# Experts on rows sorted by expert, between the two halves of the shared units

## The reference

```python
g = x @ sw1.T                                   # shared: 1024 hidden
u = x @ sw2.T
shared_out = jax.nn.silu(g) * u @ sw3.T
scores = jax.nn.sigmoid(x @ router_w.T)         # 8 experts
_, top_idx = jax.lax.top_k(scores + expert_bias, 2)
top_scores = jnp.take_along_axis(scores, top_idx, axis=-1)
top_scores = top_scores / (top_scores.sum(-1, keepdims=True) + 1e-09)
combine = jnp.zeros((T, E), x.dtype).at[jnp.arange(T)[:, None], flat_idx].add(flat_sc)
h12 = jnp.einsum('td,ehd->teh', flat_x, w12)    # 8 experts, 128 hidden each
h1, h2 = jnp.split(h12, 2, axis=-1)
out_e = jnp.einsum('teh,edh->ted', jax.nn.silu(h1) * h2, w3)
return shared_out + jnp.einsum('ted,te->td', out_e, combine).reshape(b, s, d)
```

## Time and profile before

| | |
|---|---|
| median of 3 runs | 1283.42 us (1282.84 to 1287.9) |
| profiled execution | 1282.67 us |
| its span, first to last instruction | 1280.9 us |
| TensorE (PE) busy | 1195.8 us, 93% |
| VectorE (DVE) busy | 958.9 us, 75% |
| ScalarE (ACT) busy | 577.9 us, 45% |
| GpSimd (POOL) busy | 198.2 us, 15% |
| mean granted TensorE clock | 0.962 of 2.4 GHz |

### The profile page before, as it was taken

The page is one execution under the profiler, slowest core; times in us unless marked ns, Lnnn a source line. Parts: engine busy times, 40 slices in busy tenths (PEclk is TensorE's granted clock), DMA queues, the critical chain, the costliest instruction groups (busy, mean ns, idle before and its releaser), DMA issues.

```text
span 1280.9 us, 22138 instructions
## 1 busy us (share of the span) xinstructions
PE 1195.8 (93%) x7800; PEld 798.3 (62%) x7800; DVE 958.9 (75%) x1964; ACT 577.9 (45%) x1194; POOL 198.2 (15%) x154
## 2 busy tenths in 40 slices
PE   5789999999889999999897799999999799999998
PEld 4334444444578888888783344444435688888887
DVE  7898888883558777777886688888845687777776
ACT  6236666666432232222262266676674222322322
POOL 4440000000301222222152000000003022222220
PEclk9769999999989999999987699999999899999999
DMA  3621111100100000000049423233101000000001
GB/s 127 150 41 36 36 36 36 36 12 11 61 7 26 25 25 25 25 25 0 6 119 177 58 43 65 62 66 63 23 11 59 1 26 25 25 25 25 24 0 65
DMA packets 34893, 54.59 MB, mean 43 GB/s; under 512 B 11231, under 2 KB 25503, under 8 KB 32465
## 3 DMA queue, kind: packets, MB, share of 16 engines
q1 hardware_dynamic: 31877, 41.57, 13.3%
q10 hardware_dynamic: 2940, 12.05, 4.0%
HBM read 40.94 MB, written 11.99 MB: 41 GB/s over the span
## 4 chain that ended last, share of the span: by engine, by line
PE 77%; DVE 12%; DMA 3%; ACT 2%; issue 2%; POOL 2%; SPq 1%; ACTq 0%; DVEq 0%
PE o_ps L627 11%; PE st_ps L611 10%; PE st_ps L157 8%; PE st_ps L158 8%; PE st_ps L159 8%; PE su_ps L587 6%; DVE mab L969 4%; PE st_ps L587 3%; PE o_ps L157 3%; PE su_ps L157 3%; PE o_ps L159 3%; PE su_ps L159 3%; PE o_ps L158 3%; PE su_ps L158 3%; PE st_ps L614 2%
## 5 line engine op out<-in xcount | busy, mean ns | idle before, releaser
L834 ACT ACTIVATE pt<-st_ps 128x512 f32<-128x512 f32 (+3 forms) x768 | 333.3, 494 | 225.9 <-PE st_ps L614 112.9
L611 PE MATMUL st_ps<-qs,ks 99*128 99x512 bf16 (+7 forms) x768 | 246.4, 332 | 12.2 <-DMA qs<-nmx 6.9
L157 PE MATMUL st_ps<-xt_h,wu_h 128*128 128x512 f32 x512 | 201.9, 394 | 0.0
L158 PE MATMUL st_ps<-xt_h,wu_l 128*128 128x512 f32 x512 | 201.1, 393 | 0.0
L159 PE MATMUL st_ps<-xt_l,wu_h 128*128 128x512 f32 x512 | 199.5, 390 | 0.0
L969 DVE TENSOR_REDUCE mab<-su_ps 128x1 f32<-128x512 f32 (+2 forms) x288 | 182.3, 659 | 21.0 <-PE su_ps L591 14.7
L856 ACT CAST hh<-hf 128x512 fp32r<-128x512 f32 x128 | 79.3, 620 | 227.3 <-DVE hf L1114 227.3
L1116 DVE TENSOR_TENSOR hl<-hf,hh 128x512 fp32r<-128x512 f32 x128 | 103.7, 810 | 87.8 <-ACT hh L856 87.8
L587 PE MATMUL su_ps<-ks,qs 96*128 96x512 bf16 (+5 forms) x448 | 162.5, 376 | 1.7 <-DVE mc L969 0.6
L627 PE MATMUL o_ps<-pt,vp 128*32 128x512 f32 (+3 forms) x1536 | 163.2, 498 | 0.0
L853 ACT ACTIVATE sg<-st_ps 128x512 f32<-128x512 f32 x128 | 76.5, 598 | 154.2 <-PE st_ps L159 154.2
(11 more groups left out here) (146 smaller groups left out, 1968.0 us busy)
## 6 DMA issues: line engine op xcount, KB each, us to landing
wr<-w_units_dram SPq DMA_DIRECT2D x32, 384.0 KB, 3.1
qs<-q_parts ACTq DMA_DIRECT2D x60, 128.0 KB
q_parts<-hml SPq DMA_DIRECT2D x16, 384.0 KB, 3.6
qs<-q_parts SPq DMA_DIRECT2D x36, 128.0 KB
inv<-inverses SPq DMA_DIRECT2D x128, 32.0 KB, 1.9
ks<-k_parts ACTq DMA_DIRECT2D x30, 128.0 KB
k_parts<-hml SPq DMA_DIRECT2D x8, 384.0 KB, 2.5
ks<-k_parts SPq DMA_DIRECT2D x18, 128.0 KB
```

The source lines that it names most:

```text
L157: pe.matmul(out, lh, rh, start=n == 0, stop=False)
L158: pe.matmul(out, ll, rh, start=False, stop=False)
L611: last = pe.matmul(bank[KM_BANKS[n % len(KM_BANKS)]][:, lo - CH * part:hi - CH * part], key_stack(l, s)(j)[0:rows, P * kt:P * kt + P], qs[ ...
L834: act.activation(pt[:, kt % 2, j, lo:hi], bank[KM_BANKS[i % len(KM_BANKS)]][:, lo - CH * part:hi - CH * part], ACT.Exp, scale=1 / np.sqrt( ...
```

## The change

Experts are no longer computed on all tokens. In each feed-forward:
- The steps go over chunks 0 and 1 for all 8 shared units (16 steps), then the routed part, then chunks 2 and 3 for the 8 shared units (16 steps). `down` accumulates over the 8 units in PSUM; `add_shared` adds the sum to `xs` once.
- `route` also ranks every (token, expert) pair: a count by matmul (`count_ranks`), running sums on VectorE, and so `pos`, the slot of each pair in a list in which every expert begins on a tile of 128. 4096 pairs and 8 partly filled tiles fit into 40 tiles, taken as 20 pairs of tiles (`SPAIRS`). `offset` gives the column of each tile's expert in the weights.
- POOL scatters the normalised rows into `slots` in DRAM with 32 indirect DMAs (16 tiles of tokens, 2 experts), and after the routed part gathers the rows of `outs` with 32 more; VectorE's `combine` adds each times its `share`.
- The routed part loads a pair of tiles (256 KB), transposes it, splits it, multiplies it with the weights of the experts that a register points to, applies silu and product, transposes the hidden part, splits it, multiplies again and stores the result (256 KB).
- The weights are split once, by POOL in the first attention (`keep_units`), and kept in DRAM as two parts; SyncE loads a shared unit (768 KB, ring of three) for each two steps, and both parts of all experts (6.3 MB) in each feed-forward.
- `vp` shares its place with the experts' weights, and is set to ones again by POOL after the first routed part.

The diff, cut to what the prediction speaks of:

```diff
@@ SyncE
+            def load_slots(f, i):
+                n = SPAIRS * f + i
+                if i >= 3:
+                    sp.wait_ge(rtr_done, n - 2)
+                sp.dma_start(rows_in[:, n % 3, :, :], slots_v[i]).then_inc(slots_in[n % 3], 16)
+
+            def send_outs(f, i):
+                n = SPAIRS * f + i
+                sp.wait_ge(ry_done, n + 1)
+                sp.dma_start(outs_v[i], rows_out[:, n % 3, :, :]).then_inc(outs_out[n % 3], 16)
...
+                sp.wait_ge(slots_out, 16 * 2 * TT * (f + 1))
+                for i in range(3):
+                    load_slots(f, i)
+                load_unit(f, SHARED + 2)
+                for i in range(SPAIRS):
+                    if i + 3 < SPAIRS:
+                        load_slots(f, i + 3)
+                    send_outs(f, i)
@@ POOL
+                for n in range(UNITS):
+                    pool.wait_ge(raw_in[n % 2], 16 * (n // 2 + 1))
+                    wait(pool, unit_kept, 16 * n)
+                    pool.tensor_tensor(stage[:, 0, :], wraw[:, n % 2, :], zero[:, :].to_broadcast([P, WIDTH]), ALU.subtract).then_inc(stage_step, 1)
+                    pool.wait_ge(stage_step, 2 * n + 1)
+                    pool.tensor_tensor(stage[:, 1, :], wraw[:, n % 2, :], stage[:, 0, :].bitcast(F32), ALU.subtract).then_inc(stage_step, 1)
+                    pool.wait_ge(stage_step, 2 * n + 2)
+                    pool.dma_start(unit_parts[n], stage[:, :, :].bitcast(F32)).then_inc(unit_kept, 16)
...
+            def scatter(f):
+                pool.wait_ge(pos_done, f + 1)
+                for t in range(TT):
+                    c, r = divmod(t, TC)
+                    for j in range(2):
+                        pool.indirect_dma_start(slots, bass.IndirectOffsetOnAxis(ap=pos[:, j, t:t + 1], axis=0),
+                                                normal_rows(1, c)[:, r, :], None).then_inc(slots_out, 16)
@@ TensorE
+                def turn_rows(i):
+                    n = SPAIRS * f + i
+                    pe.wait_ge(slots_in[n % 3], 16 * (n // 3 + 1))
...
+                    for a in range(2):
+                        for k in range(KE):
+                            last = pe.transpose(bank[n % 2][:, 2 * P * k + P * a:2 * P * k + P * a + P],
+                                                rows_in[:, n % 3, a, P * k:P * k + P], ident)
+                    last.then_inc(rtr_done, 1)
+
+                def up_rows(i):
...
+                    for a in range(2):
+                        at[2 * i + a] = pe.value_load(offset[0:1, 2 * i + a:2 * i + a + 1], min_val=0, max_val=WIDTH * (NEXP - 1))
+                    pe.wait_ge(rxl_done, n + 1)
+                    wait(pe, rh_done, n - 1)
+                    for a in range(2):
+                        ts = slice(P * a, P * a + P)
+                        w = at[2 * i + a]
+                        last = split_product(pe, bank[2 + n % 2][:, E * a:E * a + E], [
+                            (rx_h[:, n % 2, k, ts], rx_l[:, n % 2, k, ts], wexp_h[:, bass.ds(w + E * k, E)], wexp_l[:, bass.ds(w + E * k, E)])
+                            for k in range(KE)])
+                    last.then_inc(rup_done, 1)
...
+                for k in range(SPAIRS + 3):
+                    if k < SPAIRS:
+                        turn_rows(k)
+                    if 0 <= k - 1 < SPAIRS:
+                        up_rows(k - 1)
+                    if 0 <= k - 2 < SPAIRS:
+                        turn_hidden(k - 2)
+                    if k >= 3:
+                        down_rows(k - 3)
@@ ScalarE
+                def take_rows(i):
+                    n = SPAIRS * f + i
+                    act.wait_ge(rdown_done, n + 1)
+                    wait(act, outs_out[n % 3], 16 * (n // 3))
+                    act.copy(rows_out[:, n % 3, :, :].rearrange("p a e -> p (a e)"), bank[6 + n % 2]).then_inc(ry_done, 1)
@@ VectorE, end of a feed-forward
+                while taken < 2 * TT:
+                    combine(f, taken)
+                    taken += 1
                 if f == 0:
+                    stats(2, 0)
+                    stats(2, 1)
                     normalise(2, 0)
-                add(f, UNITS // 2 - 1, 7)
+                add_shared(f, 2)
+                add_shared(f, 3)
+                if f == 0:
+                    stats(2, 2)
+                    normalise(2, 1)
+                    stats(2, 3)
```

More of the change, by code:

```diff
@@ L48 @@
 NEXP = 8
-UNITS = 16
-FS = UNITS * NCH
+SHARED = 8
+UNITS = SHARED + NEXP
+FS = SHARED * NCH
+RING = 3
+SPAIRS = (2 * T // P + NEXP) // 2
+SLOTS = 2 * SPAIRS * P
+GBUFS = 8
+COMBINE_BEHIND = {e: 2 for e in range(19, 32)}
+WIDTH = 3 * E
+ROUTE = 2 * TT + 32
 EPS = 1e-5
@@ L297, in tr_bank, with normal_rows, unit_turn, place @@
             return bank[4 - banks + i % banks], i - banks if i >= banks else None
+        def normal_rows(p, c):
+            return xn2[:, c - 2, :, :] if p % 2 and c >= 2 else xn[:, c % 2, :, :]
+        def unit_turn(f, n):
+            return divmod(2 * SHARED * f + n, RING)
+        def place(e):
+            pair, r = divmod(e, 2 * SHARED)
+            return r // 2, 2 * pair + r % 2
+        def outs_count(n):
+            return [16 * len(range(b, n, 3)) for b in range(3)]
         def batch_parts_out(l, b, n):
@@ L421, in attention, with load_unit @@
                     sp.dma_start(wfc[:, :, :], fc_b).then_inc(wfc_in, 16)
[L423 to L427, removed]
+            def load_unit(f, n):
+                turn, r = unit_turn(f, n)
+                if n >= RING:
+                    sp.wait_ge(down_done, FS * f + 2 * (n - RING + 1))
+                sp.dma_start(wu[:, r, :, :].bitcast(F32), unit_parts[n % SHARED]).then_inc(unit_in[r], 16)
@@ L495, in _, with feed_forward @@
+            def feed_forward(f):
+                rstds(2 * f + 1)
+                scatter(f)
+                gather(f)
+            pool.wait_ge(ones_set, 2)
             rstds(0, 0, 1)
@@ new lines, in feed_forward @@
+            def feed_forward(f):
+                for e in range(2, 2 * SHARED):
+                    if e == 5:
+                        count_ranks(f)
+                    up(f, e)
+                    if e == 2:
+                        down(f, 0)
+                    down(f, e - 1)
+                down(f, 2 * SHARED - 1)
+                routed(f)
+                for e in range(2 * SHARED, FS):
+                    up(f, e)
+                    if e > 2 * SHARED:
+                        down(f, e - 1)
+                down(f, FS - 1)
@@ L1110, in hidden @@
+            def hidden(f, e):
+                s = FS * f + e
                 a = e % 2
@@ L1130, in experts, with add_shared @@
-            def experts(f):
-                for e in range(8):
-                    hidden(f, 0, e)
-                    if e:
-                        add(f, 0, e - 1)
-                    route(f, e)
-                last = UNITS // 2 - 1
-                with dve.Fori(1, last) as i:
-                    for e in range(8):
-                        hidden(f, i, e)
-                        if e:
-                            add(f, i, e - 1)
-                        else:
-                            add(f, i - 1, 7)
-                for e in range(8):
-                    hidden(f, last, e)
-                    add(f, last if e else last - 1, (e - 1) % 8)
-                    if f == 0 and e in STATS_AT:
-                        stats(2, STATS_AT.index(e))
+            def add_shared(f, c):
+                pair, r = divmod(c, 2)
+                dve.wait_ge(down_done, FS * f + 2 * SHARED * (pair + 1) - 1 + r)
+                if pair:
+                    dve.wait_ge(combined, 2 * TT * f + 2 * TC * (c + 1))
+                for half in range(2):
+                    t = TC * c + 2 * half
+                    rows = xs[:, t:t + 2, :].rearrange("p t e -> p (t e)")
+                    dve.tensor_tensor(rows, bank[4 + 2 * r + half], rows, ALU.add).then_inc(shared_added, 1)
```

501 lines of the change are left out of this document (361 added, 140 removed).

## The result

The changed kernel takes 1445.58 us (median of four runs, 1444.97 to 1449.12) where the kernel before takes 1283.13 in the same place: ratio 1.127, 95% interval [1.125, 1.129]. Its profiled execution took 1446.15 us, span 1444.2. The forecast was 1388, its 8-in-10 range 1300 to 1450.

The account below looks back on a forecast made before the run. TensorE, 93% busy, bounds the kernel before; SyncE's load-behind-send order would pace routed turns. Feed-forwards +92, tails +11.5 and splitting +2 give +105.5 us, 1388 us; forecast alone 1350 to 1430, 8 in 10 1300 to 1450.

Parts of the forecast that it names:

- The order on SyncE paces each turn: Routed part: row loads queue behind sends of results four pairs back, so sixteen turns per feed-forward pay a full round trip.
- L: Routed turn's round trip: copy with hand-overs 0.7 us, store issue 0.35, row load 3.0; sum 4.05 us, ends 3.2 and 5.2.
- TensorE at 1.2 GHz in the turns: Routed turns: gaps of 4 us leave TensorE at 1.2 GHz for nearly all its work, 5.0 us a turn.
- the routed part 177: Each feed-forward: sixteen turns of 9.8 us, 157 us, plus the first four and last turns, give 177 us, replacing 133.8.
- The rival with 2.4 GHz: Routed turns: the clock stays at 2.4 GHz, turn 7.9 us, routed part 146 us, kernel 1326 us; chance 0.25.
- Register loads: Routed part, TensorE's sequencer: two value loads a pair at 0.75 us each, 0.7 us of them bare, ends 0 and 2.2.
- Indirect DMAs at 1.27 us: First shared half, POOL: 32 scatters at 1.27 us each, 41 us in all; the gather at that cost is hidden.
- The rival of 2 us: Scatter on POOL: indirect DMAs take 2 us each, stall 27 us per feed-forward, kernel 1434 us; chance 0.15.
- the 3.7: Before the routed part: TensorE ready at 64 us, scattered rows there at 68, a stall of 3.7 us.
- The other side: Routed part: row loads hidden, turn 4.4 us, routed 92 us, kernel 1218 us; chance 0.12 of any turn below 6.5 us.
- the tail of the first layer +9.5: End of layer 0: VectorE's combines, stats and other work take 17 us where 7.5 us passed, so +9.5 us.
- Splitting beside the first attention at 2 us, ends 0 and 10: First attention: POOL's unit splitting, 152 us in all, costs 2 us through DMA traffic, ends 0 and 10.

Follow-up runs that it names:

- e1: Changed kernel with SyncE issuing the load of pair i+5, instead of i+3, ahead of the send of pair i: 1192.71 us, ratio to the kernel before 0.931.
- f2: Changed kernel with row loads issued four pairs ahead instead of three: 1237.5 us in a single execution, routed part 88.6 and 86.4 us.
- f3: e1 with fixed weight columns for each tile instead of register loads: routed part 61.7 and 61.0 us; no whole time given.
- f1: The changed kernel run again, nothing edited: 1397.48 us, ratio to the kernel before 1.089; first shared halves 70.5 and 70.5 us.
- e3: Changed kernel with only 4 of the 32 scatters per feed-forward issued: 1376.7 us in a single execution, first halves 64.6 and 64.6 us.
- f4: e1 without unit splitting, 16 transfers of zeros filling the units instead: step 2 at 384.2 us, attention 260.5 us; no whole time given.
- e4: Changed kernel with 30 of GpSimd's 32 splitting passes left out, all unit transfers kept: 1397.8 us in a single execution, attention 254.0 us.
- h1: e1 with three combines a step; layer 0 without expert loads, layer 1 with 4 of 32 scatters: 1202.54 us, ratio to the kernel before 0.936.
- g1: e1 with unit splitting and zeroing of the slots spread over the first attention: 1251.82 us, ratio to the kernel before 0.975.
- g3: e1 with splitting and zeroing spread over the first attention and three combines a step: 1249.85 us, ratio to the kernel before 0.974.

## Why the prediction was right, and where it was not

- *The order on SyncE paces each turn.* Right and shown, by e1 and f2. L was 4.05 in the forecast and is 3.7 to 4.2 in the kernel after, from the end of a result to the transposes that stand behind it.
- *TensorE at 1.2 GHz in the turns*, 5.0 us and 0.7 for register loads: 6.1 measured in the turn shown, with 0.213 us a matmul. The turn 9.8, measured 10.0; the routed part 177, measured 174.5 and 172.4. The granted clock is 0.63 in that stretch, where I had near 0.5. The rival with 2.4 GHz (7.9 a turn) did not come. Its clock came with e1, when the gap was gone.
- *Register loads*, 0.75 us each and 0.7 a pair bare: too dear. 0.30 for the load and 0.17 behind it, 0.54 bare in the turn shown, 0.37 to 0.41 a pair when warm (f3). The Trainium skill's page "DMA: Bandwidth & Descriptors", Latency and other measured facts, has a floor of about 0.6 us for such a load; the trace's median is 0.297, and the measurement decides.
- *Indirect DMAs at 1.27 us*: 0.963 and 0.30 between two in the kernel after, one each 1.28 us; 1.34 in f1, where the stall was absent. That this is so near was luck: the 1.27 was that of another operation of GpSimd. The rival of 2 us fell. They start 24 us into the steps (forecast 22.5), the rows come at 70.5 where nothing else disturbs (forecast 68). e3 gives the scatter's whole stall, 70.5 less 64.6: 5.9 us for the 3.7. The gather was hidden, as said.
- *The other side* (loads hidden, 1218): its condition did not hold, but e1 makes it hold, and then the turn is 3.24, below the 4.4 that I gave it.
- *Edges*: the tail of the first layer +9.5, measured +6.7 (from the last down to the first QKV matmul 15.5 us, by the earlier trace rows and the last down before 8.8); the last tail +2, measured +4.2.
- *Splitting beside the first attention at 2 us, ends 0 and 10*: mis-sized. 12.8 in the profile, 7.5 to 26 over twelve more. I read only the earlier trace rows and the average share of the queues, and not that three small transfers and VectorE's fixed order stand between the sums and the division. The inverses' landing went from a median of 1.9 us before to 3.5 from 88 to 166 us. That transfers alone can cause it is shown (f4), and that the passes aren't needed (e4). Why identical code lost anything from 7.5 to 26 us stays open, and that the loss goes by that round trip is argued from the waits, which name only a part.
- *What was missing*: the stall of all compute engines beside the scatter, 25 and 23 us in the two layers of the profile. With it each feed-forward is +72.6 and +70.0 where I had +46; without it, in f1, +45.8 and +47.3. The profiled execution less 47.5 us of stall is 10.6 us above the forecast, and 9.7 of them lie ahead of step 2 of the first layer, where the attention is. The same kernel takes 1397.5 us without the stall, within the 1350 to 1430 that I gave the forecast alone. The 1445.6 is outside that, by a cost that no term and no rival of mine had, 48 of the 162 us. That it still lies in the wider range, by 4 us, is luck, since that range was widened for other causes; that the routed part, the feed-forwards and the direction came out is not.

What is shown of the stall: it needs the scatters and not the expert loads (h1), and the kernel's text doesn't decide it (f1). It came in the first runs of the kernel after, in g1 to g3 and in h1's layer with 32 scatters, and in none of the seven kernels of the groups e and f that have them. Groups e, f, g and h1 ran on four chips, each group once; whether chip or loading makes the difference stays open. That the engines starve for instructions is argued: the idle time has no releaser, and comes mostly in multiples of 0.7 us between instructions of one step. The records of the instruction queue don't prove it: its 16 KB packets take 0.88 to 0.97 us beside the scatters with the stall (after) and without it (f1).

## What to carry to other kernels

Write out a queue's order with its waits, and ask for each load behind which result it stands. Buffers don't help a load that is queued behind the send of a late result, and two lines of order were worth 105 and 103 us in the two feed-forwards here and, where the stall is absent, turned +9% into -7%. And repeat the unedited kernel on another chip before an experiment is believed: three edits seemed to remove a stall that was absent from the unedited kernel too in f1, and that came back with e1's edit in place in g1 to g3.

## What the runs showed of the hardware

- The same kernel took 1445.6 us in one group and 1397.5 in another, each with a spread that excludes the other, while the kernel before, which has no indirect DMA, took 1283.1 and 1282.3.
- While 32 indirect DMAs of 128 rows of 1 KB were issued, TensorE, VectorE and ScalarE could be held back for 27 us, TensorE to 28% busy with the DMA engines at a share of 0.47 (after), to 48% over 40 us at 0.30 (h1). GpSimd took a median of 0.96 us a piece with the stall and without it (f1).
- A register load from SBUF on TensorE takes 0.297 us (median of 80, 0.295 to 0.489).
- 18 to 24 MB of bulk transfers beside the attention went with 7.5 to 26 us more for it, in twelve profiles of one execution each; with the transfers spread evenly it was 23 and 16 us.
